# Storing attention parts in their final order, and reordering the start of the last batch, in a three-stage perceiver block

## The chip, the core and the metric

The kernel runs on one core of a Trainium2 chip. The metric is device time in microseconds (us) of one execution. The kernel uses TensorE (PE, with its weight loads shown as PEld), VectorE (DVE), ScalarE (ACT), GpSimd (POOL) and the queue of SyncE (SP), from which every transfer is issued.

## What is computed

The reference is a block with three residual stages on `x` of 4 x 256 x 256, with a context of 4 x 4096 x 256:

```
x = x + xattn(layernorm(x), ctx)      # q = x Wq', k = ctx Wk', v = ctx Wv'; softmax(q k' / 16) v
                                      # out = (layernorm(x) + attended) Wo' + bo
x = x + attn(layernorm(x))            # 16 heads of 16, causal softmax; heads 0 to 2 weight a third of the keys by 1.6
x = x + soft_moe(layernorm(x))        # 64 experts x 32 slots, two softmaxes over the same logits
```

The change lies in the cross-attention, mostly in its last batch, and in how queries and keys of the self-attention reach their place.

## The kernel before, in words

The cross-attention treats four batches, each in eight chunks (`NCH`) of 512 context rows. The engines work on two batches at a time: in `batch(b)` they make the scores of batch b and, chunk by chunk, mix the probabilities of batch b-1 with the context. Every large product is made of three float32r products (high x high, low x high, high x low); ACT makes high parts, DVE and POOL low parts. After `batch(3)` comes a tail that has only the mixing of batch 3 (`LAST`) left. For each chunk in it ACT makes exponentials (`exps`), PE turns them (`transpose_probs`), ACT and DVE split them (`probs_high`, `probs_low`), and PE mixes (`mix`). Into this tail are woven the output product of batch 2 and the second layer norm's transposes. Then come four projections for the self-attention (`project_qk`, stages 0 to 3).

Each engine has its own program in a fixed order, and semaphores join them. The exponentials of a batch wait for `negmax_v` (its negated maxima) and for `sum_v`, which DVE raises in `invert_sums` once the sums of the batch before have been read.

The self-attention keeps float32 accuracy with bfloat16 by splitting queries and keys in three parts (part 0 the largest). A product of six pairs of parts is one product over 96 rows (`ROWS`), six blocks of 16 rows for 16 heads' elements. A projection stage s gives one tile of 128 x 512; ACT, DVE, ACT and POOL make its three parts, POOL the last one (`low_g`). SP stores the three parts in DRAM (`store_parts`), waits until they have landed, and loads them six times, a block of 16 partitions each, in the order of `Q_STACK` or `K_STACK` (`stack_rows`). Stages 0 to 3 are projected in the cross-attention, 4 to 7 in the first groups of the self-attention, and there PE waits for the loads of stages 4 and 5 before the scores of group 8, and for those of 6 and 7 before group 10 (L1163 is the first product of such scores). The weights `phi_w` of the third stage are loaded by the same queue behind stage 7 and turned by PE from group 8 of the loop on (L1227).

Between cross-attention and self-attention stands a block boundary: no engine passes it before all have ended the block, SP with its store of stage 3 among them.

Of the kernel before, what the change touches and what calls it, by code (L numbers as in the profile page):

```python
# [9 lines left out]
P = 128  # L10
# [3 lines left out]
QT = S // P  # L14
# [17 lines left out]
NPART = 3  # L32
Q_STACK = (0, 0, 1, 0, 2, 1)
K_STACK = (0, 1, 0, 2, 0, 1)
STACK = len(Q_STACK)
ROWS = STACK * HD
# [78 lines left out]
def store_parts(sp, kept, qk_dram, parts, s):  # L115

    rows, _ = qk_stage(s)
    sp.wait_ge(kept.sem["low_g"], s + 1)
    sp.dma_start(qk_dram[rows, s // 4].rearrange("c p t -> p c t"), parts).then_inc(kept.sem[f"parts_out{s % 2}"], 16)


def stack_rows(sp, kept, qk_dram, q_rows, k_rows, s):

    rows, _ = qk_stage(s)
    sp.wait_ge(kept.sem[f"parts_out{s % 2}"], 16 * (s // 2 + 1))
    for r in range(STACK):
        to, part = (q_rows, Q_STACK[r]) if rows < DH else (k_rows, K_STACK[r])
        sp.dma_start(to[r * HD:(r + 1) * HD, heads_of(rows), :],
                     qk_dram[rows, s // 4, part].rearrange("(i h) t -> i h t", i=HD)).then_inc(kept.sem[f"rows_in{s}"], 16)

# [65 lines left out]
def cross_attention(nc, x_sb, x_stats, x_mv, ident, kept, x, ctx, Wq, bq, Wk, bk, Wv, bv, Wo, bo,  # L196
# [5 lines left out]
    with ExitStack() as st:  # L202
# [208 lines left out]
        def _(pe):  # L411
# [86 lines left out]
            def product(e, to):  # L498
# [9 lines left out]
                last.then_inc(prod_mm, 1)  # L508

            def transpose_second(e, to):  # L510
                pe.wait_ge(h_v, TT + QT * (e + 1))
                for c in range(DH):
                    for q in range(QT):
                        last = nc.tensor.transpose(to[:, c * S + q * P:c * S + (q + 1) * P],
                                                   h2[:, QT * (e % 2) + q, c * P:(c + 1) * P], ident[:])
                last.then_inc(h2T_mm, 1)
# [91 lines left out]
            for b in range(1, B):  # L608
                batch(b)
            transpose_probs(LAST, 0, True)  # L610
            transpose_probs(LAST, 1, True)
            pe.wait_ge(scores_v, QT * NCH * B)
            for c in range(NCH):
                if c == 0:
                    transpose_attended(LAST - 1, pS[0])
                if c == 1:
                    product(LAST - 1, pS[1])
                    transpose_second(0, pS[0])
# [13 lines left out]
        def _(act):  # L632
# [47 lines left out]
            def second_turned(e, frm):  # L680
                act.wait_ge(h2T_mm, e + 1)
                nc.scalar.copy(h2T[:, :, tokens(e)], split_halves(frm[:])).then_inc(h2T_a, 1)

            def high_part(s):
                rows, _ = qk_stage(s)
                act.wait_ge(wq_a, WQ_A)
                act.wait_ge(qk2_mm, s + 1)
                nc.scalar.activation(parts(s)[:, 0, :], pS[s % 2][:], ACT.Identity, bias=kept.b_qk[:, rows:rows + 1]).then_inc(high_a, 1)
# [45 lines left out]
            for c in range(NCH):  # L734
                probs_high(LAST, c, True)
                if c == 0:
                    attended_turned(LAST - 1, pS[0])
                    act.wait_ge(w2_in, W2_IN)
                    for a in range(DH):
                        for rows in range(2 * DH):  # L740
                            cols = slice(rows * P, (rows + 1) * P)
                            nc.scalar.activation(kept.w_qkv[:, a, cols].rearrange("p (i h) -> p i h", i=HD),
                                                 w_by_head[:, a, cols].rearrange("p (h i) -> p i h", i=HD), ACT.Identity,
                                                 scale=ATT_SCALE if rows < DH else 1.0).then_inc(wq_a, 1)
                    nc.scalar.activation(kept.b_qk[:, 0:DH], kept.b_qk[:, 0:DH], ACT.Identity, scale=ATT_SCALE).then_inc(wq_a, 1)
                if c == 1:
                    second_turned(0, pS[0])
# [11 lines left out]
        def _(dve):  # L759
# [120 lines left out]
            def batch(b):  # L880
                for c in range(NCH):
# [3 lines left out]
                    if c < NCH - 1:  # L885
                        ctx_low(b, c + 1, False)
                    else:
                        maxima(b)
                        if b < LAST:
                            queries_low(b + 1)  # L890
                            ctx_low(b + 1, 0, False)
# [10 lines left out]
                ctx_high(b, NCH - 1)  # L902
                invert_sums(b - 1)
                normalise(b - 1)
# [61 lines left out]
def self_attention(nc, x_sb, x_stats, x_mv, x_ve, x_rstd, ident, kept, disp, ones, qk_dram, phi_w):  # L966
# [4 lines left out]
    with ExitStack() as st:  # L971
# [140 lines left out]
        def _(pe):  # L1112
# [118 lines left out]
            for s in range(2):  # L1231
                pe.wait_ge(rows_in[s], 16 * STACK)
            for part in range(3):
# [8 lines left out]
            for s in (2, 3):  # L1242
                pe.wait_ge(rows_in[s], 16 * STACK)
            score(2, 0)
            for i in range(GROUPS):
# [20 lines left out]
                if i + 3 < GROUPS:  # L1266
                    if i == 5:
                        for s in (4, 5):
                            pe.wait_ge(rows_in[s], 16 * STACK)
                        pe.wait_ge(frows_v, 10)  # L1270
                    if i == 7:
                        for s in (6, 7):
                            pe.wait_ge(rows_in[s], 16 * STACK)
                    score(i + 3, 0)
# [723 lines left out]
def perceiver_block(nc, x, ctx, Wq, bq, Wk, bk, Wv, bv, Wo, bo, c_attn_w, c_attn_b, c_proj_w, c_proj_b,  # L1998
                    phi_w, phi_b, expert_w, expert_b, out):
    SL = phi_w.shape[0]  # L2000
    with ExitStack() as st:
# [11 lines left out]
        bank = [st.enter_context(nc.psum_tensor(f"ps{i}", [P, 512], F32)) for i in range(8)]  # L2013
        qk_dram = nc.dram_tensor("qk_parts_dram", (2 * DH, 2, NPART, P, HALF), BF16).ap()
        phi_dram = nc.dram_tensor("phi_parts_dram", (NPART, SL), BF16).ap()
# [30 lines left out]
```

## Time and profile before

| | us |
|---|---|
| median of 3 runs (lowest to highest) | 675.2 (675.18 to 678.64) |
| the profiled execution, its own time | 674.29 |
| its span in the trace | 672.5 |
| PE busy | 608.6 (91%) |
| DVE busy | 397.4 (59%) |
| ACT busy | 347.9 (52%) |
| POOL busy | 249.5 (37%) |

The span is cut into stages by position: cross-attention from 0 to about 302.5, self-attention from about 303 to 410, the mixture of experts behind it. A row of the timeline gives the start, the duration, the engine, the line, what is written from what, and in brackets how long the engine was idle before it and what ended that. PE's busy time includes time at half the clock, so the share alone does not say how much a stage can give.

### The profile page before, as it was taken

What the parts mean: (1) busy time and instruction counts of PE and PEld (TensorE: products, weight loads), DVE (VectorE), ACT (ScalarE), POOL (GpSimd) and SP (SyncE); (2) the same over time, 40 slices, a digit from 0 to 9 for tenths busy, and PEclk for the clock granted to TensorE, in tenths of its full rate; (3) what the DMA queues carried; (4) which work ended last, traced back from release to release, by engine and by line L of the source; (5) the groups of instructions that cost most, each with busy time, mean ns of one, the idle gap of its engine ahead of it and who ended that gap; (6) DMA issues with size and microseconds to landing.
All of it is one profiled execution on the core that took longest, in us unless ns stands there. A gap on an engine that the chain in (4) does not pass through costs nothing. (4 is left out here: it accounts for less than half of the span.)

```text
span 672.5 us, 10468 instructions
## 1 busy us (share of the span) xinstructions
PE 608.6 (91%) x3740; PEld 474.9 (71%) x3740; DVE 397.4 (59%) x797; ACT 347.9 (52%) x1051; POOL 249.5 (37%) x206
## 2 busy tenths in 40 slices
PE   6998999999999998988985899899999876689998
PEld 5887999899989987866663674344448643358887
DVE  4756566666667664626774786968883578244000
ACT  2545444444444536633894783488885457741210
POOL 1442252232223243124586571333644159155000
PEclk9989999999999998998898999999999996789999
DMA  7223122112211210275188104000007048660000
GB/s 258 64 95 110 33 67 91 64 48 93 66 64 47 80 48 2 56 137 91 40 142 170 58 2 126 1 0 1 0 0 169 20 132 274 200 209 8 17 17 23
DMA packets 37000, 52.48 MB, mean 78 GB/s; under 512 B 4307, under 2 KB 31827, under 8 KB 36182
## 3 DMA queue, kind: packets, MB, share of 16 engines
q1 hardware_dynamic: 36950, 51.82, 28.2%
q8 instruction: 30, 0.49, 0.3%
q14 instruction: 20, 0.16, 0.1%
HBM read 47.60 MB, written 4.21 MB: 77 GB/s over the span
## 5 line engine op out<-in xcount | busy, mean ns | idle before, releaser
L379 POOL TENSOR_TENSOR ctx_lo<-front,ctx_hi 128x1024 fp32r<-128x1024 f32 x32 | 76.3, 2388 | 157.8 <-DVE ctx_hi L800 135.9
L485 PE MATMUL ps<-ctx_hi,pT_hi 128*128 128x256 f32 x256 | 75.5, 295 | 0.7 <-DVE pT_lo L815 0.7
L815 DVE TENSOR_TENSOR pT_lo<-ps,pT_hi 128x512 fp32r<-128x512 f32 x64 | 41.2, 686 | 56.1 <-ACT pT_hi L673 56.1
L487 PE MATMUL ps<-ctx_hi,pT_lo 128*128 128x256 f32 x256 | 72.6, 283 | 0.0
L486 PE MATMUL ps<-ctx_lo,pT_hi 128*128 128x256 f32 x256 | 72.5, 283 | 0.0
L650 ACT CAST ctxT_hi<-ps 128x512 fp32r<-128x512 f32 x64 | 34.5, 593 | 64.2 <-PE ps L442 64.2
L1711 PE MATMUL ps<-front,turned 128*128 128x512 f32 x128 | 63.5, 618 | 0.0
L1825 ACT ACTIVATE comb<-comb,cneg 128x64 f32<-128x64 f32 x160 | 62.8, 399 | 0.0
L1803 PE MATMUL ps<-front,comb 128*128 128x256 f32 x256 | 57.9, 387 | 0.0
L1658 POOL TENSOR_TENSOR disp<-disp,dinv 128x512 f32<-128x512 f32 x32 | 33.5, 1048 | 57.1 <-DVE dinv L1905 57.1
L1803 PEld LDWEIGHTS ps<-front,comb 128*128 128x128 f32 x256 | 49.5, 195 | 7.2 <-issue 0.4
L673 ACT CAST pT_hi<-ps 128x512 fp32r<-128x512 f32 x64 | 34.3, 588 | 36.0 <-PE ps L467 36.0
L485 PEld LDWEIGHTS ps<-ctx_hi,pT_hi 128*128 128x128 f32 x256 | 49.2, 192 | 1.4 <-DVE pT_lo L815 1.1
L486 PEld LDWEIGHTS ps<-ctx_lo,pT_hi 128*128 128x128 f32 x256 | 49.3, 193 | 0.1
L487 PEld LDWEIGHTS ps<-ctx_hi,pT_lo 128*128 128x128 f32 x256 | 49.1, 192 | 0.0
L792 DVE TENSOR_TENSOR ctxT_lo<-ps,ctxT_hi 128x512 fp32r<-128x512 f32 x64 | 41.2, 685 | 7.5 <-ACT ctxT_hi L650 7.1
L454 PE MATMUL ps<-ctxT_hi,qk_hi 128*128 128x512 f32 x128 | 43.0, 418 | 2.8 <-issue 2.0
L1669 POOL TENSOR_TENSOR comb<-comb,cinv 128x512 f32<-128x512 f32 x32 | 39.9, 1271 | 15.1 <-DVE cinv L1918 15.1
L1405 DVE TENSOR_REDUCE nmax<-ps 128x2 f32<-128x512 f32 (+1 forms) x48 | 31.9, 672 | 15.6 <-PE ps L1173 8.2
L454 PE MATMUL ps<-ctxT_lo,qk_hi 128*128 128x512 f32 x128 | 40.2, 396 | 0.0
L454 PE MATMUL ps<-ctxT_hi,qk_lo 128*128 128x512 f32 x128 | 40.2, 395 | 0.0
L467 PE MATMUL ps<-ident,wide 128*128 128x128 f32 x256 | 34.5, 278 | 3.7 <-ACT wide L664 3.5
(227 smaller groups left out, 1390.5 us busy)
## 6 DMA issues: line engine op xcount, KB each, us to landing
front<-in_ctx_dram SPq DMA_DIRECT2D x32, 512.0 KB, 3.3
back<-in_L_ffn_expert_w_dram SPq DMA_DIRECT2D x11, 1024.0 KB, 5.5
turned<-in_L_ffn_expert_w_dram SPq DMA_DIRECT2D x5, 1024.0 KB, 5.4
disp<-qk_parts_dram SPq DMA_DIRECT2D x24, 128.0 KB, 4.3
disp<-in_L_ffn_phi_w_dram SPq DMA_DIRECT2D x1, 2048.0 KB, 11.0
front<-in_L_ffn_expert_b_dram SPq DMA_DIRECT2D x4, 512.0 KB, 10.5
qk_parts_dram<-scores SPq DMA_DIRECT2D x4, 384.0 KB, 5.7
front<-qk_parts_dram SPq DMA_DIRECT2D x12, 128.0 KB, 4.4
```

The lines of the kernel that those rows point to most:

```text
L379: nc.gpsimd.tensor_tensor(ctx_lo[:, cols], ctx_in_sb[:, c % SLOTS, :], ctx_hi[:, cols].bitcast(F32), ALU.subtract).then_inc(split_g, 1)
L454: last = nc.tensor.matmul(pS[q][:], a[:, dh, q * P:(q + 1) * P], k[:, c % 2, dh, :], start=step == 0, stop=step == 5)
L467: last = nc.tensor.transpose(to[q][:, j * P:(j + 1) * P], probs[:, c % 2, q, j * P:(j + 1) * P], ident[:])
L485: nc.tensor.matmul(pO[q][:, 0:D], pT_hi[:, c % 2, q, cols], hi, start=c == 0 and j == 0, stop=False)
L486: nc.tensor.matmul(pO[q][:, 0:D], pT_hi[:, c % 2, q, cols], lo, start=False, stop=False)
L487: last = nc.tensor.matmul(pO[q][:, 0:D], pT_lo[:, c % 2, q, cols], hi, start=False, stop=c == NCH - 1 and j == J - 1)
L792: nc.vector.tensor_tensor(ctxT_lo[:, c % 2, dh, :], ctx_banks(c, alone)[dh][:], ctxT_hi[:, c % 2, dh, :].bitcast(F32), ALU.subtract).then_ ...
L815: nc.vector.tensor_tensor(pT_lo[:, c % 2, q, :], probs_banks(c, alone)[q][:], pT_hi[:, c % 2, q, :].bitcast(F32), ALU.subtract).then_inc(p ...
L1669: nc.gpsimd.tensor_tensor(part, part, cinv[:, c, :].unsqueeze(1).broadcast_to([P, EB, NS]), ALU.mult).then_inc(cmul_g, 1)
L1711: last = nc.tensor.matmul(psL[u % 4][:], hT[:, c, t * P:(t + 1) * P], phiT[:, c, cols], start=False, stop=c == DH - 1)
L1803: last = nc.tensor.matmul(psY[t][:, 0:HID], comb[:, t, s * P:(s + 1) * P], mixed[:, s, :], start=s == 0, stop=s == ST - 1)
L1825: nc.scalar.activation(column, column, ACT.Exp, bias=cneg[:, c, p:p + 1], accum_out=csum[:, c, p:p + 1]).then_inc(cslot_a, 1)
```

## The change

There are four edits.

1. The DRAM buffer holds six rows of parts instead of three, in the order in which they are multiplied. `store_parts` writes part r of a query tile in 3 - r places (a source that repeats), and of a key tile the parts 0 to 2, then 0 to 1, then 0: three stores for a tile instead of one. `stack_rows` loads all 96 rows with one transfer instead of six. The pairs of parts are the same, in another order.
2. DVE makes `invert_sums(b - 1)` directly behind `maxima(b)`, no longer behind two copies of the context.
3. In the tail PE makes the half of batch 2's output product that does not need the attended values (`product_of_norm`) ahead of the first transposes of probabilities; only the other half stays in chunk 1.
4. ACT reorders the weights of the self-attention in two halves, four instructions in chunk 0 and four in chunk 1, instead of eight in chunk 0.

```
-Q_STACK = (0, 0, 1, 0, 2, 1)
-K_STACK = (0, 1, 0, 2, 0, 1)
-STACK = len(Q_STACK)
+STACK = NPART * (NPART + 1) // 2
...
-    sp.dma_start(qk_dram[rows, s // 4].rearrange("c p t -> p c t"), parts).then_inc(kept.sem[f"parts_out{s % 2}"], 16)
+    first = 0
+    for r in range(NPART):
+        count = NPART - r
+        part = parts[:, r:r + 1, :].broadcast_to([P, count, HALF]) if rows < DH else parts[:, 0:count, :]
+        sp.dma_start(qk_dram[rows, s // 4, first:first + count].rearrange("r p t -> p r t"),
+                     part).then_inc(kept.sem[f"parts_out{s % 2}"], 16)
+        first += count
...
-    sp.wait_ge(kept.sem[f"parts_out{s % 2}"], 16 * (s // 2 + 1))
-    for r in range(STACK):
-        to, part = (q_rows, Q_STACK[r]) if rows < DH else (k_rows, K_STACK[r])
-        sp.dma_start(to[r * HD:(r + 1) * HD, heads_of(rows), :],
-                     qk_dram[rows, s // 4, part].rearrange("(i h) t -> i h t", i=HD)).then_inc(kept.sem[f"rows_in{s}"], 16)
+    sp.wait_ge(kept.sem[f"parts_out{s % 2}"], 16 * NPART * (s // 2 + 1))
+    to = q_rows if rows < DH else k_rows
+    sp.dma_start(to[0:ROWS, heads_of(rows), :],
+                 qk_dram[rows, s // 4].rearrange("r (i h) t -> (r i) h t", i=HD)).then_inc(kept.sem[f"rows_in{s}"], 16)
...
+            def product_of_norm(e, to):
+                for q in range(QT):
+                    rows = slice(e * S + q * P, e * S + (q + 1) * P)
+                    for c in range(DH):
+                        nc.tensor.matmul(to[:, q * D:(q + 1) * D], h1T[:, c, rows], woT[:, c, :], start=q == 0 and c == 0, stop=False,
+                                         skip_group_check=True)
...
+            pe.wait_ge(scores_v, QT * NCH * B)
+            product_of_norm(LAST - 1, pS[1])
             transpose_probs(LAST, 0, True)
             transpose_probs(LAST, 1, True)
-            pe.wait_ge(scores_v, QT * NCH * B)
...
-                    product(LAST - 1, pS[1])
+                    product_of_attended(LAST - 1, pS[1])
...
                     act.wait_ge(w2_in, W2_IN)
-                    for a in range(DH):
-                        for rows in range(2 * DH):
...
+                if c < DH:
+                    reorder_weights(c)
...
                         maxima(b)
+                        invert_sums(b - 1)
...
                 ctx_high(b, NCH - 1)
-                invert_sums(b - 1)
                 normalise(b - 1)
```

The order of DVE's instructions at the end of `batch(3)`: `csum` holds the sums by chunk, `front` the loaded context, `pT` the attended values of batch 2. First before, then of the change.

```order
L820 TENSOR_REDUCE rowmax<-cmax 128x2 [waits scores_v]
L822 TENSOR_SCALAR negmax<-rowmax 128x2 [waits max_v]
L800 CAST ctx_hi<-front 128x1024 [waits pv_mm,ctx_in2]
L800 CAST ctx_hi<-front 128x1024 [waits pv_mm,ctx_in3]
L826 TENSOR_REDUCE rowsum<-csum 128x2 [waits exp_a]
L828 RECIPROCAL rinv<-rowsum 128x2 [waits sum_v]
L835 TENSOR_SCALAR pT<-ps,rinv 128x256 [waits attT_mm,pv_mm,rinv_v]
```

And of the change:

```order
L842 TENSOR_REDUCE rowmax<-cmax 128x2 [waits scores_v]
L844 TENSOR_SCALAR negmax<-rowmax 128x2 [waits max_v]
L848 TENSOR_REDUCE rowsum<-csum 128x2 [waits exp_a]
L850 RECIPROCAL rinv<-rowsum 128x2 [waits sum_v]
L822 CAST ctx_hi<-front 128x1024 [waits pv_mm,ctx_in2]
L822 CAST ctx_hi<-front 128x1024 [waits pv_mm,ctx_in3]
L857 TENSOR_SCALAR pT<-ps,rinv 128x256 [waits attT_mm,pv_mm,rinv_v]
```

The sums and their reciprocal stand ahead of both copies, the second of which waits for PE's last mixing (`pv_mm`).

PE's instructions at the start of the tail (`wide` holds probabilities, `pT` under L495 the attended values), before:

```order
L487 MATMUL ps<-ctx_hi,pT_lo 128x256
L467 MATMUL ps<-ident,wide 128x128 [waits exp_a]
L467 MATMUL ps<-ident,wide 128x128 x3
L467 MATMUL ps<-ident,wide 128x128 [waits exp_a]
L467 MATMUL ps<-ident,wide 128x128 x3
```

And of the change, up to the same transposes:

```order
L490 MATMUL ps<-ctx_hi,pT_lo 128x256
L517 MATMUL ps<-pT,h1T 128x256 [waits scores_v]
L517 MATMUL ps<-pT,h1T 128x256 x3
L470 MATMUL ps<-ident,wide 128x128 [waits exp_a]
L470 MATMUL ps<-ident,wide 128x128 x3
```

The four products with `h1T`, the normed input, stand ahead of the first wait for exponentials.

SP's queue from the store of stage 0 to the block boundary, before:

```order
L119 DMA qk_parts_dram<-scores 128x3x512 [waits low_g]
L128 DMA front<-qk_parts_dram 16x4096 [waits parts_out0,split_g]
L128 DMA front<-qk_parts_dram 16x4096 x5
L119 DMA qk_parts_dram<-scores 128x3x512 [waits low_g]
L128 DMA back<-qk_parts_dram 16x4096 [waits parts_out1]
L128 DMA back<-qk_parts_dram 16x4096 x5
```

And of the change, of the same two stages:

```order
L121 DMA qk_parts_dram<-scores 128x3x512 [waits low_g]
L121 DMA qk_parts_dram<-scores 128x2x512
L121 DMA qk_parts_dram<-scores 128x512
L131 DMA front<-qk_parts_dram 96x4096 [waits parts_out0,split_g]
L121 DMA qk_parts_dram<-scores 128x3x512 [waits low_g]
L121 DMA qk_parts_dram<-scores 128x2x512
L121 DMA qk_parts_dram<-scores 128x512
L131 DMA back<-qk_parts_dram 96x4096 [waits parts_out1]
```

A stage has four issues instead of seven, and each load still waits for its own stores.

## Rows read from the trace of the kernel before

**Rows 1.** The page: busy tenths of the DMA engines in 40 slices of 16.8 us.

```profile
DMA  7223122112211210275188104000007048660000
```

**Rows 2.** A stretch of 2 us with mixing alone: start, length, engines busy, clock, DMA.

```profile
297.00:299.00 2.00, 2.00 (x19) 2.00 (x18) 0.00 (x0) 0.00 (x0) 0.00 (x0) 1.00 0.81 196
```

**Rows 3.** Timeline at the end of batch 3 (DVE, ACT, PE).

```profile
248.92 0.17 DVE L822 TENSOR_SCALAR negmax<-rowmax 128x2 f32<-128x2 f32 x1
250.85 1.82 DVE L800 CAST ctx_hi<-front 128x1024 fp32r<-128x1024 f32 x1 [1.16 <-PE ps L487]
252.60 0.16 DVE L826 TENSOR_REDUCE rowsum<-csum 128x2 f32<-128x16 f32 x1
252.85 0.72 ACT L664 ACTIVATE wide<-scores,negmax 128x512 f32<-128x512 f32 x1 [7.05 <-DVE rowsum L826]
253.72 3.24 PE L467 MATMUL ps<-ident,wide 128*128 128x128 f32 x16 [2.97 <-ACT wide L664]
```

**Rows 4.** Timeline of the tail's first chunks (DVE, PEld, ACT, PE).

```profile
256.29 1.29 DVE L815 TENSOR_TENSOR pT_lo<-ps,pT_hi 128x512 fp32r<-128x512 f32 x2 [2.42 <-ACT pT_hi L673]
257.63 0.29 PEld L485 LDWEIGHTS ps<-ctx_hi,pT_hi 128*128 128x128 f32 x1 [0.22 <-DVE pT_lo L815]
258.33 2.62 ACT L742 ACTIVATE w_qkv<-front 128x128 f32<-128x128 f32 x8
261.81 1.36 PE L467 MATMUL ps<-ident,wide 128*128 128x128 f32 x8 [0.56 <-ACT wide L664]
263.00 1.03 PE L504 MATMUL ps<-pT,h1T 128*128 128x256 f32 x4
266.46 0.60 PE L514 MATMUL ps<-ident,pT 128*128 128x128 f32 x4
```

**Rows 5.** Timeline of POOL, SP's queue and PE around the block boundary.

```profile
278.60 1.17 POOL L407 TENSOR_TENSOR scores<-scores 128x512 bf16<-128x512 f32 x1 [9.32 <-ACT scores L692]
279.80 0.36 SPq L119 DMA_DIRECT2D qk_parts_dram<-scores  x1
282.39 2.65 SPq L128 DMA_DIRECT2D front<-qk_parts_dram  x6
294.49 1.17 POOL L407 TENSOR_TENSOR scores<-scores 128x512 bf16<-128x512 f32 x1 [3.81 <-ACT scores L692]
302.09 0.42 SPq L119 DMA_DIRECT2D qk_parts_dram<-scores  x1
303.16 0.58 PE L1163 MATMUL ps<-back,front 99*128 99x128 bf16 x4 [3.75 <-PEq L202]
315.02 0.39 PE L1163 MATMUL ps<-back,front 96*128 96x128 bf16 x4
```

**Rows 6.** Stretches of 1 us: start, length, five engines busy, clock, DMA share, GB/s.

```profile
281.00:282.00 1.00, 1.00 (x10) 0.88 (x9) 0.12 (x1) 0.62 (x2) 0.00 (x0) 1.00 0.88 296
304.00:305.00 1.00, 1.00 (x6) 0.64 (x5) 0.64 (x2) 0.00 (x0) 0.55 (x1) 0.50 1.08 131
370.00:371.00 1.00, 1.00 (x9) 0.70 (x6) 0.09 (x1) 0.95 (x6) 0.00 (x0) 0.50 1.08 346
```

**Rows 7.** Timeline of SP, POOL and PE in the self-attention.

```profile
331.70 0.38 SPq L119 DMA_DIRECT2D qk_parts_dram<-qk_parts  x1
347.23 1.16 POOL L1073 TENSOR_TENSOR qk_parts<-qk_rest,qk_parts 128x512 bf16<-128x512 f32 x1 [0.77 <-ACT qk_parts L1322]
350.47 0.39 PE L1163 MATMUL ps<-disp 99*128 99x128 bf16 x4 [1.22 <-DMA disp<-qk_parts_dram]
359.72 2.62 SPq L128 DMA_DIRECT2D disp<-qk_parts_dram  x6
367.67 0.58 PE L1163 MATMUL ps<-disp 96*128 96x128 bf16 x4 [7.81 <-DMA disp<-qk_parts_dram]
373.44 0.66 PE L1227 MATMUL ps<-ident,disp 128*128 128x128 f32 x4 [0.62 <-DMA disp<-in_L_ffn_phi_w_dram]
```

**Rows 8.** Timeline of PE behind the ends of batches 1 and 2.

```profile
125.30 0.66 PE L495 MATMUL ps<-ident,pT 128*128 128x128 f32 x4 [0.82 <-DVE pT L835]
```

More of the change, by code:

```diff
@@ L508, in product, with product_of_attended @@
                 last.then_inc(prod_mm, 1)
+            def product_of_norm(e, to):
[4 more added lines that the diff above has]
+                                         skip_group_check=True)
+            def product_of_attended(e, to):
+                pe.wait_ge(attT_a, e + 1)
+                for q in range(QT):
+                    for c in range(DH):
+                        last = nc.tensor.matmul(to[:, q * D:(q + 1) * D], attT[:, c, q * P:(q + 1) * P], w2[:, c, :],
+                                                start=False, stop=c == DH - 1, skip_group_check=True)
+                last.then_inc(prod_mm, 1)
             def transpose_second(e, to):
@@ L682, in second_turned, with reorder_weights @@
                 nc.scalar.copy(h2T[:, :, tokens(e)], split_halves(frm[:])).then_inc(h2T_a, 1)
+            def reorder_weights(a):
+                for rows in range(2 * DH):
+                    cols = slice(rows * P, (rows + 1) * P)
+                    nc.scalar.activation(kept.w_qkv[:, a, cols].rearrange("p (i h) -> p i h", i=HD),
+                                         w_by_head[:, a, cols].rearrange("p (h i) -> p i h", i=HD), ACT.Identity,
+                                         scale=ATT_SCALE if rows < DH else 1.0).then_inc(wq_a, 1)
             def high_part(s):
@@ L738, in _ @@
                     act.wait_ge(w2_in, W2_IN)
-                    for a in range(DH):
-                        for rows in range(2 * DH):
[L741 to L744, printed above, removed]
                     nc.scalar.activation(kept.b_qk[:, 0:DH], kept.b_qk[:, 0:DH], ACT.Identity, scale=ATT_SCALE).then_inc(wq_a, 1)
+                if c < DH:
+                    reorder_weights(c)
                 if c == 1:
@@ L1231, in _ @@
             for s in range(2):
-                pe.wait_ge(rows_in[s], 16 * STACK)
+                pe.wait_ge(rows_in[s], 16)
             for part in range(3):
@@ L1242, in _ @@
             for s in (2, 3):
-                pe.wait_ge(rows_in[s], 16 * STACK)
+                pe.wait_ge(rows_in[s], 16)
             score(2, 0)
@@ L1268, in _ @@
                         for s in (4, 5):
-                            pe.wait_ge(rows_in[s], 16 * STACK)
+                            pe.wait_ge(rows_in[s], 16)
                         pe.wait_ge(frows_v, 10)
@@ L1272, in _ @@
                         for s in (6, 7):
-                            pe.wait_ge(rows_in[s], 16 * STACK)
+                            pe.wait_ge(rows_in[s], 16)
                     score(i + 3, 0)
@@ L2013, in perceiver_block @@
         bank = [st.enter_context(nc.psum_tensor(f"ps{i}", [P, 512], F32)) for i in range(8)]
-        qk_dram = nc.dram_tensor("qk_parts_dram", (2 * DH, 2, NPART, P, HALF), BF16).ap()
+        qk_dram = nc.dram_tensor("qk_parts_dram", (2 * DH, 2, STACK, P, HALF), BF16).ap()
         phi_dram = nc.dram_tensor("phi_parts_dram", (NPART, SL), BF16).ap()
```

## The prediction

> **What bounds the kernel now.** I began with the page's slices [rows 1]: the DMA engines are loaded in slices 17 to 22 (about 270 to 370 us), where the stored parts travel. Stretch by stretch, PE is full in the cross-attention's tail (a stretch of mixing alone has 19 products at work in 2 us, two or three of them begun before it, so they start 0.12 apart [rows 2]). The timelines then show three holes of PE in the region of the change. A reader should see in each what ended it.
>
> - End of batch 3 [rows 3]: PE's last mixing ends at 250.75 (253.72 less 2.97), and PE stands until ACT has an exponential. ACT had been idle for 7.05 us; what it lacked was `rowsum`, and DVE reached that only at 252.60, behind a copy that began when PE's mixing was over and took 1.82 us. The maxima were there at 249.09.
> - Block boundary [rows 5]: PE stands 3.75 us until 303.16. POOL finished the parts of stage 3 at 295.66, but SP stored them only at 302.09, since its queue was behind. All engines waited for that.
> - Groups 8 to 10 [rows 7]: 1.22 us for the loads of stages 4 and 5, 7.81 us for those of 6 and 7, and 0.62 for `phi_w` behind them.
>
> From chunk 3 of the tail on PE is the bound (POOL's stages come (294.49 - 278.60) / 3 = 5.3 us apart [rows 5], PE's work of a chunk), so what is won at its start stays won.
>
> **The parts, against the profiled execution (674.29).**
>
> *Sums early.* Behind `negmax` (248.92) the sums start at about 249.1 and ACT at 249.25 instead of 252.85. The moved pair, 0.16 and about 0.2 us with its wait, pushes the copy in front of it back by 0.4; the second copy starts at 250.85 as before, may end 0.4 later, and saves the 0.4 of the pair behind it. So the attended values of batch 2 come at 254.0, as before. The new order on PE from 250.75: product of the norm, 1.73 us (half of 263.00 to 266.46 [rows 4]), 16 transposes in 1.75, so 254.2, four more for the attended values to 255.1 (0.11 each, an estimate from the four in 0.66 with their drain [rows 8]). ACT has made four exponentials by 252.1 (0.71 each) and casts to 254.1; DVE is free at 254.0 and takes 1.29 [rows 4] for the low parts: 255.35. Mixing of chunk 0 then starts at 255.4, not 257.63 [rows 4]: 2.2 us. What bounds it next is DVE's low part.
>
> *Chunk 0.* PE's mixing is 24 products at 0.12, 2.9 us; before it took 3.6 (257.63 to 261.25, where PE's idle 0.56 begins), and the clock was low at its start, as behind the other holes [rows 6]. Then PE waited for exponentials that stood behind eight reorderings (2.62 us): its transposes came at 261.81 and ended at 263.00. With four reorderings (1.31) ACT's second exponential is ready at 258.5, PE's transposes end at 259.2. That is 3.8 ahead, 1.6 more than 2.2. The second four fall where ACT waits for PE in chunk 1.
>
> *Product halved.* In chunk 1 PE has 1.73 us less to do, since the norm's half lies in what was the hole. Sum at the start of chunk 1's mixing: 2.2 + 1.6 + 1.7 = 5.5 us. If the hole were not there, moving would bring nothing. Bounds: 3.5 (the copy's delay repeats and the clock still falls) and 6.
>
> *Two earlier batch ends.* Behind batches 1 and 2 PE has its scores to do while it waits, but DVE's attended values come 0.4 earlier without the pair in front; PE waits 0.82 for them [rows 8], twice in the same pattern. 0.4 x 2 = 0.8 us. Bounds 0 and 1.6.
>
> *Stores and loads.* This is the large term, and its price hangs on one number that the trace doesn't have: how long the new load of 96 rows x 8 KB (786 KB) occupies the DMA engines, L. The model is a chain through one queue. A store of 393 KB was issued at 279.80 and had landed at 282.39 [rows 5]; at 296 GB/s [rows 6] its transfer is 1.33 us, the rest 0.87 before it and 0.4 behind. Six loads of 16 partitions (786 KB) run at 131 GB/s [rows 6]: 6.0 us, with the engines at a full share. A store now moves 786 KB, 2.66 us if it keeps 296; three issues cost 1.2 us of SP, of which all but the first lie under the first's transfer; the load's single issue is 0.45 where six took 2.65.
> For L the nearest rows pull apart: 131 GB/s for 16 partitions (6.0 us), 346 GB/s for `phi_w` over 128 partitions [rows 6] (2.3 us). In both the engines are at a full share, so it is the spread over partitions that differs, and 96 is nearer to 128. I take 2.8, a little above the lower end, because 96 rows fall unevenly.
> The page SBUF — State Buffer of the Trainium skill, section Door 1: The DMA port swizzle, says the same with a mechanism: 16 neighbouring partitions reach 4 of 16 ports, 96 reach all, eight of them doubly loaded. By the rate of a port here (131 / 4 = 33 GB/s, an estimate) the doubly loaded ones would need 2.0 us for their 64 KB; the sum with that would be about 1.5 us lower.
>
> With L = 2.8 the chain of stages 0 to 3, from POOL's times less the common shift: store 0 lands 283.7, load 0 ends 287.4, store 1 lands 290.4, load 1 ends 294.1, store 2 lands 297.1, its load is issued at 297.2 and store 3 by 298.9. PE ends at about 299.3, so PE now bounds the block. Before, PE began 1.07 us behind the start of SP's last issue (302.09 to 303.16), 0.65 behind its end; 299.2 + 0.65 = 299.85, 3.3 us gained. Bounds: L = 2.3 the same, L = 3.3 gives 2.6, L = 6 loses 2.8.
>
> *Clock behind the boundary.* The hole of 3.75 us took PE to half clock (0.50 in 304 to 305 [rows 6]). From 303.16 to 315.02 PE is the bound: 11.9 us. With a pause of 0.6 it should stay at full clock; the scores then take 1.2 instead of 2.2 and the transposes 0.5 less: 1.5 us. Bounds 0 and 1.7.
>
> *Stages 4 to 7.* POOL ends the four stages from 331.7 (SP's store starts there) to 348.4, 5.6 apart [rows 7]. The same chain: loads land at 339.7, 346.5, 353.2 and 359.9; `phi_w` (2 MB at 346 GB/s, 6.05 us) follows at 366.0. PE needs stage 5 at 349.25: there. It asks for stages 6 and 7 at 359.86, less the 1.22, so at 358.6, and goes on at 359.9. One group later (5.15 us in the trace, at half clock; 3.3 at full, an estimate) it asks for `phi_w`, at 363.2, and waits until 366.0, where it waited until 373.44: 7.4 us. So `phi_w` is late next, and the 7.8 us hole doesn't close wholly. Bounds: L = 2.3 gives 9.4, L = 3.3 gives 5.4, L = 6 loses 5.3.
>
> Checked against what it should reproduce, the same chain with 1.33 and 6.0 puts the last loads of before at 367.5 (PE went on at 367.67).
>
> *Sum.* 5.5 + 0.8 + 3.3 + 1.5 + 7.4 = 18.5 us, so 655.8 for an execution like the profiled one. The median lies 0.9 above that execution: 656.7. What comes later (experts, 410 us on) starts from these points and has no timer of its own, so I carry the gain to the end.
>
> **Rivals.**
>
> A. The load is faster, but only to some 175 GB/s (L = 4.5), because engines meet at a partition group while they walk. SP's end is 302.3, gain 0.2; no gain of clock; `phi_w` at 372.8, gain 0.6. With 6.3 from the tail: 7.1 us, 668. For it: no row lies between 131 and 346, so the middle is open. Against: 96 partitions are three quarters of those that gave 346.
>
> B. The transfers are as forecast, but the tail gives half: POOL's subtraction (2.36 us) again holds DVE's copy, ACT's chain becomes the bound, PE's clock falls all the same. 3 us instead of 6.3, 660.
>
> C. The single load keeps 131 GB/s. Tail +6.3, boundary -2.8, `phi_w` -5.3: 1.8 us slower than the profiled execution, about 677. It is what would happen if the transfer were not spread over all 16 engines.
> DMA: Bandwidth & Descriptors of the Trainium skill, section Why a DMA increments its semaphore by 16 and not by 1, says that a transfer uses as many engines, up to 16, as divide the slowest dimension of both sides. The DRAM side could be read as 6 x 16 x 8; if 6 were the slowest, six engines would run at 346 / 16 = 22 GB/s each, an estimate of 6.0 us, rival C. The order prints 96 x 4096 for the load, and 96 divides by 16, which speaks against it.
>
> D. Slower: twice the stored bytes in one queue with loads that gain nothing, or lose. From L = 6.5 (120 GB/s) the boundary costs 3.8 and `phi_w` 7.3, together 4.8 more than the tail gives: 680. It decides from L = 6.3. A row of 96 gives each engine six partitions in turn, so all might press on few partition groups at a time. Against: 131 with 16 partitions in reach should be the floor.
>
> That the change does nothing is hardly possible: the waits it removes are in the trace.
>
> **How the numbers follow.** Forecast (L 2.3 to 3.3, tail whole): 0.60, 654 to 661. A 0.15, B 0.14, C 0.06, D 0.05. The predicted time is 656.7. The range: 651 takes in L = 2.0 with all upper bounds, 668 takes in B and A; C and D, 0.11, are left out. A measurement of this kernel can tell about 0.5%, 3.4 us. Faster: forecast, A and B, 0.89. Same: C, 0.06. Slower: D, 0.05.
>
> **What would show it.** Load: a stretch of 1 us in which a load runs alone near 280 GB/s, landing under 4.5 us after its issue. Tail: `rowsum` directly behind `negmax`, PE's idle time before the first transposes under 0.5 us, the second four reorderings in ACT's idle time. Boundary: under 1 us of idle PE, clock 1.00 behind it. Group 10: the long wait at L1163 gone, a wait of 2 to 3 us for `phi_w` in its place. Wrong if the loads still run at 131 GB/s, or if the engines wait at the boundary for SP.

## The result and the profile after

The changed kernel takes 664.93 us in the median of 4 runs (663.54 to 666.16), the kernel before 675.19 in runs beside it (674.3 to 678.64). The ratio is 0.9838, 95% interval 0.9803 to 0.9874: 10.3 us or 1.6% faster. The time lies in the predicted range of 651 to 668, but outside the 654 to 661 of the forecast itself; the gain is 8.2 us short of the point. The profiled execution took 666.16, the slowest of the four (span 664.4), so its own gain over 674.29 is 8.1.

The page of the kernel after, issues with KB each and us to landing:

```profile
PE 609.1 (92%) x3740; PEld 476.2 (72%) x3740; DVE 398.5 (60%) x797; ACT 347.8 (52%) x1051; POOL 249.6 (38%) x206
...
DMA  7123121211221120372278004000007148670000
...
HBM read 47.60 MB, written 7.35 MB: 83 GB/s over the span
...
disp<-qk_parts_dram SPq DMA_DIRECT2D x4, 768.0 KB, 5.9
...
disp<-in_L_ffn_phi_w_dram SPq DMA_DIRECT2D x1, 2048.0 KB, 11.2
...
front<-qk_parts_dram SPq DMA_DIRECT2D x2, 768.0 KB, 5.5
```

The DMA engines' slices 17 to 22, where the parts travel, hold 3 7 2 2 7 8 tenths where [rows 1] has 2 7 5 1 8 8. PE is as busy as before, in a span 8.1 us shorter. A load of 96 rows lands 5.5 to 5.9 us after its issue (medians of the groups), where the forecast asked for under 4.5.

The timeline of the kernel after in the cross-attention (start, length, engine, line, in brackets the idle time before it):

```profile
126.49 0.66 PE L498 MATMUL ps<-ident,pT 128*128 128x128 f32 x4 [0.41 <-DVE pT L857]
...
249.69 0.17 DVE L844 TENSOR_SCALAR negmax<-rowmax 128x2 f32<-128x2 f32 x1
249.77 0.16 DVE L848 TENSOR_REDUCE rowsum<-csum 128x2 f32<-128x16 f32 x1
...
250.03 0.73 ACT L683 ACTIVATE wide<-scores,negmax 128x512 f32<-128x512 f32 x1 [3.45 <-DVE rowsum L848]
...
251.36 1.89 PE L517 MATMUL ps<-pT,h1T 128*128 128x256 f32 x8
...
251.63 2.11 DVE L822 CAST ctx_hi<-front 128x1024 fp32r<-128x1024 f32 x1 [0.89 <-PE ps L490]
...
253.09 1.91 PE L470 MATMUL ps<-ident,wide 128*128 128x128 f32 x16
...
255.78 0.39 PE L488 MATMUL ps<-ctx_hi,pT_hi 128*128 128x256 f32 x1 [0.34 <-DVE pT_lo L837]
...
256.06 1.37 ACT L706 ACTIVATE w_qkv<-front 128x128 f32<-128x128 f32 x4
...
258.76 1.04 PE L470 MATMUL ps<-ident,wide 128*128 128x128 f32 x8
...
261.72 0.36 PE L488 MATMUL ps<-ctx_hi,pT_hi 128*128 128x256 f32 x1
```

The first line answers to [rows 8]: PE waits 0.41 us less for the attended values. The rest answers to [rows 3] and [rows 4]: the sums stand directly behind the maximum, ACT starts 0.34 us behind `negmax` instead of 3.93, and PE's 2.97 us hole is full of the norm's product. Counted from `negmax`, chunk 0's mixing begins 6.09 us later, where it was 8.71. The four reorderings lie in front of chunk 1's exponentials without holding PE.

The same timeline around the boundary and in the self-attention (SP's queue and PE):

```profile
274.71 1.55 SPq L121 DMA_DIRECT2D qk_parts_dram<-scores  x3
...
278.45 0.33 SPq L131 DMA_DIRECT2D front<-qk_parts_dram  x1
...
285.53 0.33 SPq L131 DMA_DIRECT2D back<-qk_parts_dram  x1
...
293.51 0.33 SPq L131 DMA_DIRECT2D front<-qk_parts_dram  x1
293.88 2.14 SPq L121 DMA_DIRECT2D qk_parts_dram<-scores  x3
...
296.70 0.39 PE L1185 MATMUL ps<-back,front 99*128 99x128 bf16 x4 [2.40 <-PEq L205]
...
325.15 1.44 SPq L121 DMA_DIRECT2D qk_parts_dram<-qk_parts  x3
...
330.43 0.33 SPq L131 DMA_DIRECT2D disp<-qk_parts_dram  x1
...
344.51 0.39 PE L1185 MATMUL ps<-disp 99*128 99x128 bf16 x4 [1.82 <-DMA disp<-qk_parts_dram]
...
354.55 0.33 SPq L131 DMA_DIRECT2D disp<-qk_parts_dram  x1
354.92 0.43 SPq L1066 DMA_DIRECT2D disp<-in_L_ffn_phi_w_dram  x1
...
360.43 0.59 PE L1185 MATMUL ps<-disp 96*128 96x128 bf16 x4 [3.73 <-DMA disp<-qk_parts_dram]
...
366.41 0.60 PE L1249 MATMUL ps<-ident,disp 128*128 128x128 f32 x4
```

They answer to [rows 5] and [rows 7]. PE waits for SP again at the boundary, 2.40 us instead of 3.75. SP's loads are issued 8 us apart (285.53 to 293.51; 330.43 to 354.55 in three steps), where the forecast's chain has 6.7. PE waits 3.73 us at the loads of stages 6 and 7, and not at all for `phi_w`.

Stretches of the kernel after (start, length, five engines busy, clock, DMA share, GB/s):

```profile
286.50:293.00 6.50, 6.50 (x53) 6.07 (x52) 2.28 (x5) 2.87 (x5) 2.43 (x2) 1.00 0.87 240
...
298.00:299.00 1.00, 1.00 (x7) 0.94 (x6) 1.00 (x3) 0.00 (x0) 0.07 (x1) 0.50 0.86 304
...
302.00:303.00 1.00, 1.00 (x6) 0.90 (x5) 0.00 (x0) 1.00 (x6) 0.72 (x1) 1.00 0.86 139
303.00:304.00 1.00, 1.00 (x6) 0.87 (x6) 0.29 (x2) 0.21 (x2) 0.50 (x1) 1.00 0.82 303
304.00:305.00 1.00, 1.00 (x7) 0.87 (x6) 1.00 (x4) 0.00 (x0) 1.00 (x1) 1.00 1.04 254
305.00:306.00 1.00, 1.00 (x6) 0.90 (x5) 0.96 (x5) 0.00 (x0) 0.60 (x2) 1.00 0.43 107
...
350.00:351.00 1.00, 1.00 (x6) 0.68 (x5) 0.05 (x1) 0.00 (x0) 0.00 (x0) 0.50 0.70 204
```

Against [rows 6]: the load of stage 3, alone in the queue from 302 to 306, reaches 303 GB/s where six loads had 131, but its whole transfer takes 3.5 us (302.0 to 305.5, 229 GB/s in the mean), not 2.8, and it lands 5.2 us after its issue, 1.0 behind its last byte. The first row holds a load and the three stores issued right behind it: together 1.57 MB in 6.5 us, where the forecast had 2.8 and 2.66, so 5.5. Behind the boundary and behind the wait at 344.51 the clock is at 0.50, the lower of its two levels.

### The profile page after: what moved, and what is told of

Same layout as the page of the kernel before. It is cut to its first block and busy times, and to the rows that moved or that the text cites. A ratio compares the mean times of both kernels' runs of the same rounds, so it can differ in the third digit from the quotient of the medians.

```text
span 664.4 us, 10443 instructions
## 1 busy us (share of the span) xinstructions
PE 609.1 (92%) x3740; PEld 476.2 (72%) x3740; DVE 398.5 (60%) x797; ACT 347.8 (52%) x1051; POOL 249.6 (38%) x206
## 5 line engine op out<-in xcount | busy, mean ns | idle before, releaser
L1825 PE MATMUL ps<-front,comb 128*128 128x256 f32 x256 | 56.2, 379 | 0.0
L1427 DVE TENSOR_REDUCE nmax<-ps 128x2 f32<-128x512 f32 (+1 forms) x48 | 31.8, 672 | 14.4 <-PE ps L1195 11.2
L1733 PEld LDWEIGHTS ps<-front,turned 128*128 128x128 f32 x128 | 22.0, 192 | 23.2 <-issue 23.2
## 6 DMA issues: line engine op xcount, KB each, us to landing
disp<-in_L_ffn_phi_w_dram SPq DMA_DIRECT2D x1, 2048.0 KB, 11.2
```

What stands on the lines that cost most here:

```text
L1733: last = nc.tensor.matmul(psL[u % 4][:], hT[:, c, t * P:(t + 1) * P], phiT[:, c, cols], start=False, stop=c == DH - 1)
L1825: last = nc.tensor.matmul(psY[t][:, 0:HID], comb[:, t, s * P:(s + 1) * P], mixed[:, s, :], start=s == 0, stop=s == ST - 1)
```

## The experiments

Start-up differs by some us between executions of any of these kernels (the kernel after is 1.19 us behind at 126.49 and 0.77 at `negmax`). So the executions are compared from `negmax` of batch 3 on, in five parts: A to SP's first store of parts; B to PE's first product of the self-attention; C to the first store of stage 4; D+E to the first product of the experts, D ending at PE's wait for the rows of stages 6 and 7. "6 to 7" is the time from the store of stage 6 to that of stage 7. All in us, from one profiled execution each.

| kernel | A | B | hole at the end of B | C | D | D+E | sum | 6 to 7 |
|---|---|---|---|---|---|---|---|---|
| before | 30.88 | 23.36 | 3.75 | 28.54 | 35.97 | 79.12 | 161.90 | 9.75 |
| after | 25.02 | 21.99 | 2.40 | 28.45 | 35.28 | 78.76 | 154.22 | 7.92 |
| after_again | 25.01 | 21.99 | 2.38 | 26.76 | 34.64 | 78.34 | 152.10 | 8.04 |
| tail_only | 25.00 | 23.43 | 3.83 | 28.60 | 36.08 | 79.32 | 156.35 | 9.47 |
| sums_only | 27.63 | 23.57 | 3.97 | 29.14 | 35.50 | 78.98 | 159.32 | 9.84 |
| product_only | 28.29 | 23.09 | 3.48 | 29.72 | 36.47 | 79.82 | 160.92 | 9.95 |
| stores_only | 30.89 | 21.48 | 1.88 | 27.19 | 35.21 | 78.25 | 157.81 | 7.97 |
| six_loads | 25.00 | 28.89 | 9.29 | 28.86 | 42.99 | 86.30 | 169.05 | 10.85 |
| three_loads | 25.02 | 23.64 | 4.05 | 28.68 | 36.79 | 80.52 | 157.86 | 9.43 |
| two_loads | 25.00 | 22.72 | 3.13 | 28.69 | 35.62 | 78.88 | 155.29 | 8.71 |
| run_loads | 25.00 | 20.09 | 0.48 | 26.89 | – | 74.80 | 146.78 | 6.34 |
| run_phi | 25.00 | 20.07 | 0.48 | 26.92 | 31.04 | 73.37 | 145.36 | 6.96 |
| fill | 24.99 | 22.03 | 0.45 | 26.80 | – | 78.47 | 152.29 | 8.08 |
| phi_early | 25.02 | 21.47 | 1.87 | 27.17 | 34.80 | 77.98 | 151.64 | 8.01 |

A dash stands where PE no longer waited for those rows.

The theory after the result: the tail did all that was forecast; the load takes longer than 2.8 us and its landing more than 0.4, so SP's chain stays the limit. The rivals: that the clock took the gain, that the tail gave less and the transfers more, or that the doubled store costs it.

**The two halves of the change: tail_only and stores_only.** Edits 2 to 4 without edit 1, and edit 1 alone.

```
tail_only, stores as before:
-STACK = NPART * (NPART + 1) // 2
+Q_STACK = (0, 0, 1, 0, 2, 1)
+K_STACK = (0, 1, 0, 2, 0, 1)
...
```

> Edits 2 to 4 alone (sums, product, reordering); stores and loads as before. Theory 1, the tail's gain of about 6 us is whole and passes to the end because everything behind it only shifts: 668.5 to 669.5, SP's store of stage 3 still last at the boundary with PE idle 3.7 us, the 7.8 us wait at group 10 unchanged. Rival, half of the tail's gain is swallowed by SP's queue, which runs on its own time: 672 or more.

> Edit 1 alone (three stores in final order, one load of 96 rows); tail as before. Theory 1, the two parts add up: the whole change is 10.3 below before, so 671 to 672, period of SP's stages 8.0 us, landing of the load 5.2 to 6.0 us behind its issue. Rival, the parts work only together (an earlier tail is what lets SP's queue be ahead): 674 to 675.

tail_only: 669.39 (666.66 to 670.5), ratio 0.9891 [0.9852, 0.9929]. stores_only: 672.89 (669.53 to 676.3), 0.9957 [0.9923, 0.9991]. The kernel before stood at 676.66 (669.6 to 677.76). tail_only came out as its theory had it, with 3.83 us of idle PE at the boundary and 7.93 at the rows of stages 6 and 7. stores_only lies between its theory (671 to 672) and its rival (674 to 675); its parts A to E are those of the theory, with a cycle of 7.97. The tail's gain is all in A, 5.88 us; the stores' is 1.88 in B, 1.35 in C, 0.87 in D+E. The sums of the two are -5.55 and -4.09, together 9.6, where the profiled execution of the change has 7.7 and its repetition 9.8. The two parts add up within what the repetition leaves open. So most of the real gain is the tail's, which was forecast as a third of it.

**The doubled store with the old loads: six_loads.** The store in the final order, read back in six pieces of 16 partitions.

```
-    sp.dma_start(to[0:ROWS, heads_of(rows), :],
-                 qk_dram[rows, s // 4].rearrange("r (i h) t -> (r i) h t", i=HD))...
+    for r in range(STACK):
+        sp.dma_start(to[r * HD:(r + 1) * HD, heads_of(rows), :],
+                     qk_dram[rows, s // 4, r].rearrange("(i h) t -> i h t", i=HD))...
```

> The whole change, but the 96 rows are loaded by six transfers of 16 partitions each, out of the same stored rows. Theory 1, the spread over partitions is what made the load faster: 131 GB/s again, period of a stage 10 us or more, 673 to 677, slower than the change by 8 or more. Rival, it is the number of transfers and not their spread that costs: rate near 230 GB/s also with six, 665 to 668.

684.13 (682.17 to 688.59), 1.0141 [1.009, 1.0193], slower than even the theory's 673 to 677. Its timeline has the longest holes of all, and in a microsecond with one of its loads alone the rate is 131 GB/s:

```profile
305.17 0.58 PE L1186 MATMUL ps<-back,front 99*128 99x128 bf16 x4 [9.29 <-PEq L206]
...
377.02 0.59 PE L1186 MATMUL ps<-disp 96*128 96x128 bf16 x4 [9.45 <-DMA disp<-qk_parts_dram]
...
284.00:285.00 1.00, 1.00 (x11) 1.00 (x10) 0.75 (x1) 1.00 (x3) 0.00 (x0) 1.00 1.10 131
```

Between tail_only, this kernel and the after, the change's two effects come apart. Doubling the store costs 5.46 us in B and 6.91 in D; loading in one piece brings back 6.90 and 7.71. Over D's four stages that is 1.7 us for a store, forecast at 1.33, and 1.9 us for a load, forecast at 3.2. What was to be 1.9 us net for each stage became 0.2. The loads of tail_only show the same 131 GB/s (297 to 301), so reading the six rows from places of their own does not slow the loads. Whether the dearer store is a matter of its bytes or of its three transfers, no run separates.

**One load in two or three pieces: three_loads and two_loads.** The same store, loads of 48, 32 and 16 partitions, or of 64 and 32.

```
+    first = 0
+    for count in (3, 2, 1):      # two_loads: (4, 2)
+        sp.dma_start(to[first * HD:(first + count) * HD, heads_of(rows), :],
+                     qk_dram[rows, s // 4, first:first + count]...
+        first += count
```

> The change with its three stores (786 KB), and the 96 rows loaded by three transfers of 48, 32 and 16 partitions as in run_loads. The stretch from the maxima of batch 3 to the experts was 161.9 us before, 154.2 with the change, 146.8 in run_loads. Theory 1, run_loads won by its smaller store (1.33 us less of transfer and two issues less for each stage), not by the shape of its loads: 154 to 156 here. Rival, a load in three pieces is itself the faster one: 150 or less.

> The change, its load cut in two of 64 and 32 partitions. Theory 1 (engines that walk six partitions each meet at the same partition group now and then; with four and two partitions each they meet evenly, 131 GB/s for each 16 partitions in reach, up to 262): the load takes 3.0 us instead of 3.4 to 3.9, the stretch is 1 to 2.5 us shorter than 154.2. Rival, the time is that of reading 8 KB pieces from DRAM whatever the cut: 154 to 155.

One run each, 669.48 and 667.2, beside 676.8 for the kernel before. Both expectations of my theory were too low: with three pieces the sum is 157.86 (theory 154 to 156, rival 150 or less), with two 155.29, beside the rival's figure. That two even pieces would suit the engines better is not borne out. In both the clock fell behind the boundary, but B, which ends ahead of that, grows all the same: 21.99 for one piece, 22.72, 23.64, and 28.89 for six. Splitting the load never helped; the whole load is the best of the four forms tried of reading the final order.

**A compact store and loads by runs: run_loads.** This goes back to the compact store, with about as many loads as three_loads: one store of 393 KB, and loads that take runs of neighbouring parts (0 to 2, 0 to 1, 0 for queries; 0 to 1, 0 to 1, 0, 2 for keys), the same pairs of parts.

```
+Q_RUNS = ((0, 3), (0, 2), (0, 1))
+K_RUNS = ((0, 2), (0, 2), (0, 1), (2, 1))
...
+    sp.dma_start(qk_dram[rows, s // 4].rearrange("c p t -> p c t"), parts)...
...
+    for first, count in runs:
+        sp.dma_start(to[r * HD:(r + count) * HD, heads_of(rows), :],
+                     qk_dram[rows, s // 4, first:first + count].rearrange("r (i h) t -> (r i) h t", i=HD))...
+        r += count
```

> The whole change, but the parts are stored once (393 KB, one store) and loaded in runs of neighbouring parts: three transfers of 48, 32 and 16 partitions for queries, four of 32, 32, 16 and 16 for keys (the six products in another order). Theory 1, the time of a stage is set by bytes and landings in one queue: 1.33 us of store instead of 2.66 and a load of 3.5 to 4, period 6.3 instead of 8.0, the boundary bound by PE, last loads 5 us earlier: 659 to 661. Rival, a load over fewer partitions loses as much as the store wins (5 us or more for a load): 664 to 667.

662.44 (656.25 to 665.33), 0.982 [0.9786, 0.9854], against the before above; between theory and rival; the cycle of 6.34 is the theory's. The profiled execution is the fastest of its five, and its sum is 7.4 us below that of the after and 11.1 below that of three_loads. By the times alone run_loads and the after can't be told apart: their intervals overlap. With the load split in the same way, the compact store saves 3.55 us in B and 5.72 in D+E. So the doubled store is the price: what one large load gives, it takes back.

**Holes filled: fill.** PE makes transposes that nobody reads, 18 at the end of the cross-attention, 16 and 32 ahead of the two waits for rows.

```
+            for _ in range(18):
+                nc.tensor.transpose(bank[0][:, 0:P], ident[:], ident[:])
```

> The whole change, with extra transposes of the identity on PE just ahead of its three waits (18 ahead of the block boundary, 16 ahead of the wait for stages 4 and 5, 32 ahead of that for 6 and 7; a transpose starts every 0.11 us), written to memory that is overwritten. Theory 1, the holes cost their length only once more through the clock: full clock behind the boundary gives 1.6 us there, and the rest nothing, since the last loads land on SP's time anyway: 1.5 to 2 us under the change. Rival, the clock costs at every hole: 2.8 us more behind stages 4 and 5 and some 2 behind 6 and 7, together 5 or more.

666.46 (662.1 to 668.04), 0.9849 [0.979, 0.9909], beside 674.83 (670.44 to 679.85): by its times no gain over the change, whose ratio is 0.9838. In the profiled execution C is 26.80, 1.65 us below the after, and the sum 1.9 below. I first took that for a proof that the clock had eaten 1.9 us of the change. It isn't one:

**The change once more: after_again.** No edit.

> The change itself once more, for how well the stretch from the maxima of batch 3 to the experts repeats, when the whole time scatters by 2 us. Theory 1, what scatters lies in the first 250 us (the first loads): 154.2 within 0.5. Rival, it lies in SP's queue and the clock: off by 1 or more.

664.44 (one run). The rival was right. The stretch behind the boundary, of the after first, then of the same kernel again:

```profile
297.70:299.70 2.00, 2.00 (x12) 1.82 (x10) 1.84 (x3) 0.30 (x1) 0.37 (x1) 0.55 0.93 313
299.70:301.70 2.00, 2.00 (x7) 1.62 (x6) 0.18 (x1) 2.00 (x11) 0.01 (x1) 0.60 0.36 124
```

```profile
297.76:299.76 2.00, 2.00 (x16) 1.83 (x14) 1.83 (x3) 0.95 (x4) 0.36 (x1) 1.00 0.90 310
299.76:301.76 2.00, 2.00 (x11) 1.77 (x10) 0.18 (x1) 2.00 (x11) 0.67 (x1) 1.00 0.32 110
```

And the timeline of the repetition:

```profile
296.76 0.39 PE L1185 MATMUL ps<-back,front 99*128 99x128 bf16 x4 [2.38 <-PEq L205]
...
310.42 0.38 PE L1185 MATMUL ps<-back,front 96*128 96x128 bf16 x4 [1.90 <-ACT eA L1355]
...
342.71 0.39 PE L1185 MATMUL ps<-disp 99*128 99x128 bf16 x4 [1.65 <-DMA disp<-qk_parts_dram]
...
358.16 0.59 PE L1185 MATMUL ps<-disp 96*128 96x128 bf16 x4 [6.19 <-DMA disp<-qk_parts_dram]
```

Behind a hole of 2.40 us the clock fell to 0.50, behind one of 2.38 it stayed at 1.00, and C is 1.69 us shorter. The gain of 1.5 us forecast for the clock is of the right size, and comes in some executions only. fill, at 152.29, does no better than the repetition at 152.10. The clock then kept its full level behind the wait at 342.71 too; PE came to the rows of stages 6 and 7 earlier and stood 6.19 us for them. D shrank by 0.64 alone: there it is SP's chain that sets the time, whatever PE's clock is.

**The last weights earlier: phi_early and run_phi.** The load of `phi_w` is issued right behind the load of stage 3 instead of behind stage 7, in the change and in run_loads.

```
             stack_rows(sp, kept, qk_dram, *first_rows(kept), 3)
+            sp.dma_start(phi_nat, phi_w.rearrange("(k p) d -> p k d", p=P)).then_inc(phi_in, 16)
...
-            sp.dma_start(phi_nat, phi_w.rearrange("(k p) d -> p k d", p=P)).then_inc(phi_in, 16)
```

> The change, with the load of phi_w issued at the start of the self-attention. In the change's trace the rows of stages 6 and 7 land at 360.35, phi_w at 366.1, and PE, at half clock, asks for it just then. Theory 1, phi_w is not what binds there: 0 to 1 us. Rival, by the prediction's step it is next in line: 2 us or more.

> As run_loads, and the load of phi_w is issued at the start of the self-attention, behind stage 3's loads, when the DMA engines have nothing to do for 25 us, no longer behind stage 7. Theory 1, in run_loads PE waited 2.43 us for phi_w alone: 2 to 2.5 us under run_loads, 12 to 13 under the change in the stretch from the maxima of batch 3 to the experts. Rival, the wait moves to the rows of stages 6 and 7, which land just as late: under 1 us.

phi_early: one run, 664.87; its sum is 0.5 us below the repetition's, but B, which ends ahead of the edit, is shorter by that much too; in D+E, where the edit acts, it is 0.36. So `phi_w` hardly binds in the change, as expected. run_phi: 658.4 (655.9 to 660.73, 6 runs), 0.9747 [0.9702, 0.9792], with 674.83 beside it. Its sum is 1.4 us below run_loads', where PE had waited 2.43 us for `phi_w`; 2 to 2.5 were expected, and 12 to 13 below the after's, where it is 8.9. It beats both kernels: 2.5% below the one before, and its interval lies wholly under that of the change. From its timeline:

```profile
288.18 0.42 SPq L119 DMA_DIRECT2D qk_parts_dram<-scores  x1
...
293.43 1.23 SPq L129 DMA_DIRECT2D front<-qk_parts_dram  x3
...
294.70 0.42 SPq L119 DMA_DIRECT2D qk_parts_dram<-scores  x1
...
354.66 0.38 PE L1189 MATMUL ps<-disp 96*128 96x128 bf16 x4 [1.20 <-DMA disp<-qk_parts_dram]
...
361.03 0.66 PE L1253 MATMUL ps<-ident,disp 128*128 128x128 f32 x4 [1.18 <-DVE front L1453]
```

SP's stores stand 6.5 us apart, PE's wait for the last rows is 1.20 us, and the product with `phi_w` waits for DVE instead of a transfer.

**The tail's two edits apart: sums_only and product_only,** each alone on the kernel before.

```
sums_only:
                         maxima(b)
+                        invert_sums(b - 1)
product_only:
+            product_of_norm(LAST - 1, pS[1])
             transpose_probs(LAST, 0, True)
```

> Edit 2 alone (the sums behind the maxima). From the maxima of batch 3 to SP's first store of parts it is 30.9 us before and 25.0 with the whole tail. Theory 1 by the working: 2.2 us of the 5.9, so 28.5. Rival, without the split reordering ACT's exponentials are late again and most of it is lost: 30 or more.

> Edit 3 alone (the norm's half of the product ahead of the transposes, with the sums still late). Theory 1: the hole of 3.0 us takes the 1.7 us of product, the same stretch is 1.7 us shorter, 29.2, and PE's clock doesn't fall, 0.5 more. Rival, the product only delays the transposes and nothing is won: 30.9.

One run each, 676.95 and 674.78 beside 674.83: start-up and clock drown a part of this size, so only A is read. It falls by 3.25 for the sums and 2.59 for the product. Both are more than expected (2.2, and 1.7 with 0.5 for the clock). The clock matters in both: in the kernel before it is 0.50 from 256 to 258, in both single-edit kernels it stays at 1.00, and chunk 0's mixing takes 3.1 us instead of 3.6 in each. That half microsecond is therefore counted twice in the 5.84 that the two make together, so its nearness to the 5.86 of all three edits does not show that the reorderings in halves give nothing. In both kernels PE still waits for exponentials behind eight reorderings (0.41 and 0.16 us, 0.56 before), and in the after it doesn't. No run leaves out edit 4 alone: its share is open.

## Why the prediction was right in part and wrong in size

By the prediction's own steps, predicted and measured, from the profiled executions of before and after (in brackets the repetition):

| step | predicted | measured |
|---|---|---|
| batch ends | 0.8 | 0.8 |
| tail (A) | 5.5 | 5.86 (5.87) |
| boundary (B) | 3.3 | 1.37 (1.37) |
| clock behind it (C) | 1.5 | 0.09 (1.78) |
| stages 4 to 7, `phi_w` (D+E) | 7.4 | 0.36 (0.78) |

To these come a start-up 1.6 us later in the profiled after, and experts 1.2 us shorter (261.7 to 260.5); neither is touched by the change. The measured column, -1.6 and +1.2 give 8.1, the difference of the spans. That the median still lies within 651 to 668 is owed to the upper end, which was drawn to take in rivals A and B; the largest term was missed by 7 us.

- **Batch ends, right.** The lag of 1.6 at the start is 0.77 at `negmax`; the wait shown fell by 0.41, as worked out, and that of the next batch from 0.83 to 0.41.
- **Tail, right.** Chunk 1's mixing begins 12.03 us behind `negmax` where it was 17.90: 5.87, forecast 5.5. DVE's low part bounds chunk 0, as forecast, and it comes 2.6 instead of 2.2 earlier. From there to the output product it is 3.85 us (255.78 to 259.63) instead of 5.37 (257.63 to 263.00): 1.5, forecast 1.6; the halved product gives 1.73, forecast 1.7. So the split by stretches holds. Which edit earned it is another matter: of the 1.5, 0.64 is chunk 0's mixing at full clock, of which either of the other two edits brings 0.5 alone, and the part of the four reorderings was not measured.
- **Stores and loads: this step failed,** and by sizes, not by mechanism. The step took L as 2.8 us (281 GB/s) from the neighbourhood of 346 GB/s, a landing 0.4 us behind, and a second half of the store for 1.33. The load exceeded that rate, with 303 GB/s, in its best microsecond only and took 3.5 us alone; it lands 5.5 to 5.9 us after its issue, where 4.1 was in the chain. The chain from the first store of stage 4 to the last rows is 35.28 us instead of 28.2, barely under the 35.97 of before. The 7.1 us are made up so: 1.35 in the store of stage 4, which takes 5.28 us to the issue of its load and not 3.93, with nothing else in the queue; 3 x 1.3 in the three cycles, 8.0 instead of 6.7, of which 1.0 is the longer transfer of load and store together; 1.8 in the last load. At the boundary the same excess took 1.9 us of the forecast 3.3, and the queue of SP, not PE, stayed the bound there: that was one of the prediction's own signs of being wrong. (By [rows 5] PE's work before it ended at 303.16 - 3.75 = 299.41, not 299.2, so that 3.3 was 0.2 too high from the start.) My upper case L = 3.3 would have kept 5.4 of the 7.4: the error isn't in L alone, the store and the landings around it hold as much.
- **The check of the chain was no test of it.** It reproduced the before within 0.2 us with one store of 393 KB and loads that fill the queue longer than any landing; the terms that the change adds were not in it.
- **Clock, right in size, but not to be had for certain.** I required a hole of 0.6 us; it was 2.40 and in the repetition 2.38, and the clock fell in one execution and not in the other.
- **`phi_w` late next: wrong.** It lands 11.2 us after its issue at 354.92, so at 366.1, and PE asks for it at 366.41. Since the rows of stages 6 and 7 came late, it was just in time. In run_loads, where they came early, the wait is there as forecast, 2.43 us: the order of what binds was right, for another kernel.
- **Rival A** (L = 4.5, 668) is the nearest to what happened in B and D+E: it gave the boundary 0.2 and `phi_w` 0.6. Its rate was too low, 175 GB/s against 229, and its reason, engines that meet at a partition group, no run shows. Rivals B to D are out: the tail gave all, and the loads don't run at 131.
- The port rule of the Trainium skill (SBUF — State Buffer, section Door 1: The DMA port swizzle) was right in direction: loads of 16 partitions ran at 131 GB/s, one of 96 at 229. The estimate of 2.0 us that I worked out with it was too low against 3.5; and by the step's own slope (L = 2.3 gives 9.4 instead of 7.4) the sum would be 3.2 us lower with it, not 1.5.
- The page DMA: Bandwidth & Descriptors of the Trainium skill, section Why a DMA increments its semaphore by 16 and not by 1, could be read so that six engines are at work. The 303 GB/s, at an engine share of 0.82, refute that reading.

What stays open: why load and store together take 1.0 us more than forecast, and why the doubled store of stage 4 takes so long with nothing in front of it. In seven of the eight profiles with the doubled store it takes 5.05 to 5.29 us to the issue of its load (4.15 in fill), in the kernels with the compact store 2.48 or 2.49; at stage 0 it is 3.7 against 2.6. In the after nearly all of its data has moved by 328.5, 3.3 us after the first issue, and the load is issued only at 330.43.

## What to carry to other kernels

In a chain of store, landing and load through one queue, count each byte and each landing on the path: here a layout that made the load one transfer won 1.9 us a stage and lost 1.7 by doubling what the store has to write. Look first for a middle way (here runs of neighbouring parts) that widens the load and leaves the store alone. And repeat a profile before a microsecond or two is put down to the clock.

## What the runs showed of the hardware that was not expected

- One kernel, two executions, holes of PE of 2.40 and 2.38 us: granted clock 0.50 behind the one, 1.00 behind the other. Over the 14 profiles C is 26.8 to 27.2 behind holes of 0.45 to 2.38 us, and 28.4 to 29.7 behind holes of 2.40 to 9.29.
- The three stores at the head of a chain take 1.44 to 1.55 us of SP, those of stage 3, issued right behind a load, 2.14. The place alone doesn't decide it: in fill the stores of stage 4, at the head too, take 2.29.
- Of a load of 786 KB that is read from the same DRAM tile, one piece over 96 partitions is faster than two, three or six, though its rate swings from one microsecond to the next (139, 303 and 254 GB/s).
